# Top-2 experts: the routing weight multiplied into the gate's activation by GpSimd, all 16 down products in one PSUM bank

## What is computed

```python
def moe(x2d, W_router, gate_w, up_w, down_w):
    logits = x2d @ W_router.T
    probs = jax.nn.softmax(logits.astype(jnp.float32), -1)
    topw, sel = jax.lax.top_k(probs, TOPK)
    topw = topw.astype(x2d.dtype)
    wmat = jnp.sum(jax.nn.one_hot(sel, E, dtype=x2d.dtype) * topw[..., None], axis=1)
    g = jnp.einsum('td,efd->tef', x2d, gate_w)
    u = jnp.einsum('td,efd->tef', x2d, up_w)
    h = jax.nn.silu(g) * u
    ye = jnp.einsum('tef,edf->ted', h, down_w)
    out = jnp.einsum('ted,te->td', ye, wmat)
    return (out, logits)
```

## Time and profile before

| what | value |
|---|---|
| median of 3 runs | 1696.12 us (1695.65 to 1700.82) |
| profiled execution, its own time | 1696.32 us |
| span from first to last instruction | 1694.5 us |
| mean granted TensorE clock | 0.826 of full speed |
| TensorE matmul busy | 1251.0 us (74%) |
| VectorE busy | 1175.1 us (69%) |
| ScalarE busy | 606.9 us (36%) |
| GpSimd busy | 395.3 us (23%) |

### The profile page before, as it was taken

How to read it: one execution, slowest core, us unless ns; L and a number is a source line. 1 busy time by engine, 2 the same in 40 slices (tenths; PEclk the granted TensorE clock), 3 DMA queues, 4 the chain that set the end, 5 groups by cost and what they waited for, 6 DMA issues and landing times.

```text
span 1694.5 us, 13336 instructions
## 1 busy us (share of the span) xinstructions
PE 1251.0 (74%) x4026; PEld 619.1 (37%) x4026; DVE 1175.1 (69%) x2595; ACT 606.9 (36%) x1086; POOL 395.3 (23%) x284
## 2 busy tenths in 40 slices
PE   2222775966487675967696887878889789999897
PEld 1001332332233222343232553635547345555554
DVE  6897798878987898847547688696785752444321
ACT  1510652236322642224232331412233325764543
POOL 5232042312422142211103223030320111111211
PEclk8555886979697986969797679797787989999999
DMA  5000000000000000020001000000000010000000
GB/s 178 0 0 0 1 1 0 1 0 1 0 1 1 0 0 1 1 85 1 1 0 56 1 1 0 1 1 1 1 1 1 0 56 1 7 1 7 1 7 7
DMA packets 11271, 17.78 MB, mean 10 GB/s; under 512 B 1304, under 2 KB 7584, under 8 KB 10688
## 3 DMA queue, kind: packets, MB, share of 16 engines
q1 hardware_dynamic: 11200, 16.93, 2.9%
HBM read 15.88 MB, written 1.05 MB: 10 GB/s over the span
## 4 chain that ended last, share of the span: by engine, by line
PE 33%; DVE 14%; ACT 4%; issue 2%; POOL 1%; POOLq 0%; DVEq 0%; ACTq 0%
PE bankE L1659 7%; PE bankE L1737 4%; PE bankE L1149 4%; PE bankE L1132 3%; DVE b_yt L1454 2%; PE bankE L1151 1%; PE bankS L1701 1%; PE bankE L518 1%; PE bankS L1686 1%; ACT b_pr L1046 1%; DVE c_tw L1829 1%; PE bankE L544 1%; DVE b_xnS L1236 1%; PE bankE L1134 1%; DVE b_pT L1426 1%
## 5 line engine op out<-in xcount | busy, mean ns | idle before, releaser
L284 POOL TENSOR_TENSOR cv<-cv,hc 128x1024 f32<-128x1024 f32 x60 | 141.4, 2357 | 303.9 <-DVE hc L683 303.6
L676 DVE TENSOR_TENSOR_SCAN hs<-dA,carry,dbx 128x512 f32<-128x512 f32 x128 | 186.0, 1493 | 3.9 <-ACT dA L358 0.5
L1659 PE MATMUL bankE<-c_h,c_w 128*128 128x512 f32 x288 | 151.7, 609 | 9.5 <-DVE c_tw L1829 6.6
L1632 ACT ACTIVATE c_h<-bankE,C 128x512 f32<-128x512 f32 x144 | 98.9, 688 | 117.4 <-PE bankE L1737 117.2
L395 ACT ACTIVATE sg<-bankE,C 128x512 f32<-128x512 f32 x80 | 54.9, 687 | 172.5 <-PE bankE L518 172.5
L1829 DVE SCALAR_TENSOR_TENSOR c_tw<-bankE,C,wb_ready 128x512 f32<-128x512 f32 x32 | 24.0, 750 | 130.0 <-PE bankE L1659 130.0
L449 PE MATMUL bankS<-bc,sel 96*128 96x512 bf16 x64 | 30.5, 476 | 102.5 <-DVE hc L683 89.5
L1737 PE MATMUL bankE<-c_fH,c_w1H 128*128 128x512 f32 x144 | 100.8, 700 | 0.0
L1046 ACT ACTIVATE b_pr<-bankE,b_nm 128x160 f32<-128x160 f32 x128 | 48.4, 404 | 139.3 <-DVE b_nm L1415 139.3
L1149 PE MATMUL bankE<-b_kTt,b_qT 64*128 64x160 f32 x256 | 85.9, 424 | 9.4 <-ACT b_pr L1046 8.8
L358 ACT ACTIVATE dA<-dl,Aneg 128x512 f32<-128x512 f32 x128 | 81.1, 709 | 26.6 <-DVE hs L676 26.4
(11 more groups left out here) (478 smaller groups left out, 2829.3 us busy)
## 6 DMA issues: line engine op xcount, KB each, us to landing
c_w<-in_w SPq DMA_DIRECT2D x1, 2304.0 KB, 8.7
X<-in_x SPq DMA_DIRECT2D x4, 256.0 KB, 3.8
wg<-in_gate_T SPq DMA_DIRECT2D x1, 1024.0 KB, 7.9
wu<-in_up_T SPq DMA_DIRECT2D x1, 1024.0 KB, 10.0
f<-in_w SPq DMA_DIRECT2D x1, 1024.0 KB, 7.3
out<-X SPq DMA_DIRECT2D x4, 256.0 KB, 2.3
b_wq<-in_Wqkv SPq DMA_DIRECT2D x1, 768.0 KB, 4.9
g<-in_sw SPq DMA_DIRECT2D x2, 256.0 KB, 3.5
```

The costliest lines, as they stand in the source:

```text
L284: pool.tensor_tensor(cv[:, :, :], cv[:, :, :], hc[:, k % 2, :, :], ALU.add).then_inc(s["y_acc"], 1)
L676: V.tensor_tensor_scan(hs[:, h, :], dA[:, (HV * k + h) % DA, :], dbx[:, h, :], carry[:, k, h:h + 1], ALU.mult, ALU.add).then_inc(s["scan_d ...
L1632: act.activation(h[:, n % 3, :], E[k % 2][:, :], ACT.Gelu_apprx_tanh, bias=col("b1_3", k)).then_inc(s["c_h"], 1)
L1659: pe.matmul(E[2][:, :], w2[:, k, :], h[:, n % 3, :], start=(f == 0), stop=(f == FB3 - 1)).then_inc(s["c_down"], 1)
```

## The change

- `weigh`, `add`, the tile tw and the semaphore tw_ready are gone. GpSimd multiplies each of the 16 blocks' sg with its expert's wb in place, piece by piece, and signals sw_ready; VectorE's hh now waits for sw_ready in place of sg_ready.
- sg has three buffers in place of two. ScalarE writes wb for expert x once GpSimd has multiplied all blocks up to expert x-2.
- TensorE accumulates all 16 down products in E[2], and ScalarE copies the sum to acc in L1.
- ORDER is written anew from aA0.1 on, in all stages. The pieces are the same ones.
- Six waits and signals that ran on semaphores of their own now count on shared ones (acts_const, x2_done, b_cst, b_room), with the counts raised to match.

The order around the M blocks, old and then new (expert groups 0, 1, 2 and the tail):

```diff
@@ -93,49 +93,49 @@
...
-    aA0.1 an0.1 ao0.1 aM5.0 aN1.1 aM6.0 an1.1 aM7.0 ao1.1 aM8.0 aN2.1 aM9.0 an2.1 ao2.1 aN3.1 aA1.1 an3.1 ao3.1 aM10.0 aN4.1 aM11.0 an4.1
-    ao4.1 aM12.0 aN5.1 aM13.0 an5.1 aM14.0 ao5.1 aM15.0 aN6.1 aL1.0 an6.1 aA2.1 aL3.0 ao6.1 aL4.0 aN7.1 aL5.0 an7.1 aR2.0 ao7.1 aR5.0 aN8.1
...
-    aF3.2 aM1.1 aM2.1 aF8.2 aF4.2 aF9.2 aM3.1 aM4.1 aN0.2 aA0.2 an0.2 ao0.2 aM5.1 aN1.2 aM6.1 an1.2 aM7.1 ao1.2 aM8.1 aN2.2 aM9.1 an2.2
-    ao2.2 aM10.1 aN3.2 aM11.1 aA1.2 an3.2 ao3.2 aN4.2 an4.2 ao4.2 aM12.1 aN5.2 aM13.1 an5.2 aM14.1 ao5.2 aM15.1 aN6.2 an6.2 aL1.1 aA2.2
...
-    aF1.3 aR1.2 aF5.3 aR3.2 aF6.3 aF2.3 aF0.3 aR4.2 aF7.3 aM0.2 aF3.3 aM1.2 aM2.2 aF8.3 aF4.3 aF9.3 aM3.2 aM4.2 aN0.3 aA0.3 an0.3 ao0.3
-    aM5.2 aN1.3 an1.3 aM6.2 ao1.3 aM7.2 aN2.3 an2.3 ao2.3 aN3.3 aA1.3 an3.3 ao3.3 aM8.2 aN4.3 aM9.2 an4.3 aM10.2 ao4.3 aM11.2 aN5.3 an5.3
...
-    aU18.2 aU19.2 aB1.3 aL2.2 aL6.2 aB3.3 aB4.3 aB2.3 aL7.2 bP0.0 aR1.3 aR3.3 bP1.0 aR4.3 aM0.3 aM1.3 bP2.0 bP3.0 bP4.0 bK1.0 aM2.3 aM3.3
-    bK11.0 aM4.3 aM5.3 bK2.0 bK3.0 bK13.0 aM6.3 aM7.3 bK4.0 aM8.3 aM9.3 bK14.0 aM10.3 bK5.0 aM11.3 bK8.0 aM12.3 bK15.0 aM13.3 aM14.3 aM15.3
...
+    aA0.1 an0.1 ao0.1 aM5.0 aN1.1 aM6.0 aM7.0 an1.1 aM8.0 ao1.1 aM9.0 aN2.1 aM10.0 aM11.0 an2.1 aM12.0 ao2.1 aM13.0 aN3.1 aM14.0 aM15.0
+    aL1.0 aA1.1 an3.1 aL3.0 ao3.1 aL4.0 aN4.1 aL5.0 an4.1 aR2.0 ao4.1 aR5.0 aN5.1 aR6.0 an5.1 ao5.1 aU0.0 aN6.1 an6.1 aU1.0 aA2.1 ao6.1
...
+    aF7.2 aM0.1 aF3.2 aM1.1 aM2.1 aF8.2 aF4.2 aF9.2 aM3.1 aM4.1 aN0.2 aA0.2 an0.2 ao0.2 aM5.1 aN1.2 aM6.1 an1.2 aM7.1 ao1.2 aN2.2 an2.2
+    aM8.1 ao2.2 aN3.2 aA1.2 an3.2 ao3.2 aM9.1 aN4.2 aM10.1 an4.2 aM11.1 ao4.2 aM12.1 aN5.2 aM13.1 an5.2 aM14.1 ao5.2 aN6.2 an6.2 aM15.1
...
+    aB2.2 aF1.3 aF5.3 aF6.3 aF2.3 aF0.3 aL7.1 aF7.3 aR1.2 aF3.3 aF8.3 aR3.2 aR4.2 aF4.3 aF9.3 aM0.2 aM1.2 aN0.3 aA0.3 an0.3 ao0.3 aM2.2
+    aN1.3 aM3.2 an1.3 aM4.2 ao1.3 aM5.2 aN2.3 aM6.2 aM7.2 an2.3 aM8.2 ao2.3 aN3.3 aA1.3 an3.3 aM9.2 aM10.2 ao3.3 aN4.3 aM11.2 an4.3 aM12.2
...
+    aU16.2 aU17.2 aB1.3 aB3.3 aB4.3 aU18.2 aU19.2 aB2.3 bP0.0 aL2.2 aL6.2 bP1.0 aL7.2 bP2.0 bP3.0 bP4.0 bK1.0 aR1.3 bK11.0 aR3.3 bK2.0 aR4.3
+    bK3.0 bK13.0 aM0.3 aM1.3 aM2.3 aM3.3 aM4.3 aM5.3 aM6.3 aM7.3 aM8.3 aM9.3 aM10.3 aM11.3 aM12.3 aM13.3 bK4.0 aM14.3 aM15.3 bK14.0 aL1.3
...
```

The rest of the diff; the renamed semaphores of stages b and c are of the same kind as the ones in `scalar`:

```diff
@@ -210,10 +210,10 @@
...
     c3 = sb2("c3", [E1N, G], BF16)
-    sg = sb2("sg", [P, 2, G])
+    SG = 3
+    sg = sb2("sg", [P, SG, G])
     hh = sb2("hh", [P, 2, G])
     wb = sb2("wb", [P, 2, G])
-    tw = sb2("tw", [P, 2, G])
     acc = sb2("acc", [P, G])
@@ -284,12 +284,10 @@
...
                 power("s_var", "s_pow", powS, rsS, i, 2, 3)
-            elif p[0] == "M" and int(p[1:]) % FB0 == FB0 - 1:
-                x_ = int(p[1:]) // FB0
-                if x_ > 0:
-                    add(e, x_ - 1)
-            elif p == "L1":
-                add(e, E0N - 1)
+            elif p[0] == "M":
+                at_least(pool, s["sg_ready"], e, N_M, k + 1)
+                at_least(pool, s["wb_ready"], e, E0N, k // FB0 + 1)
+                pool.tensor_tensor(sg[:, k % SG, :], sg[:, k % SG, :], wb[:, k // FB0 % 2, :], ALU.mult).then_inc(s["sw_ready"], 1)
             elif p == "L3":
@@ -297,25 +295,16 @@
...
-        def add(e, x_):
-
-            at_least(pool, s["tw_ready"], e, E0N, x_ + 1)
-            if x_ == 1:
-                pool.tensor_tensor(acc[:, :], tw[:, 0, :], tw[:, 1, :], ALU.add).then_inc(s["acc_done"], 1)
-            elif x_ > 1:
-                at_least(pool, s["acc_done"], e, E0N - 1, x_ - 1)
-                pool.tensor_tensor(acc[:, :], acc[:, :], tw[:, x_ % 2, :], ALU.add).then_inc(s["acc_done"], 1)
-
         return piece
...
         act.wait_ge(s["ld_x"], 32)
-        act.activation(Aneg[:, :], col("A_log", 0, HV * NS), ACT.Exp).then_inc(s["act_self"], 1)
-        act.wait_ge(s["act_self"], 1)
+        act.activation(Aneg[:, :], col("A_log", 0, HV * NS), ACT.Exp).then_inc(s["acts_const"], 1)
+        act.wait_ge(s["acts_const"], 1)
         act.activation(Aneg[:, :], Aneg[:, :], ACT.Copy, scale=-1.0).then_inc(s["acts_const"], 1)
         act.activation(sb2sum[:, :], col("sb2", 0), ACT.Identity, bias=col("sb2", 1)).then_inc(s["acts_const"], 1)
-        act.wait_ge(s["acts_const"], 2)
+        act.wait_ge(s["acts_const"], 3)
         act.wait_ge(s["consts"], 4)
@@ -371,13 +360,15 @@
...
                     at_least(act, s["wbc_ready"], e, E0N, x_ + 1)
-                    if x_ >= 2:
-                        at_least(act, s["tw_ready"], e, E0N, x_ - 1)
+                    at_least(act, s["sw_ready"], e, N_M, max(0, FB0 * (x_ - 1)))
                     act.activation(wb[:, x_ % 2, :], E[3][:, :], ACT.Copy).then_inc(s["wb_ready"], 1)
                 at_least(act, s["g_ready"], e, N_M, k + 1)
-                if k >= 2:
-                    at_least(act, s["hh_ready"], e, N_M, k - 1)
-                act.activation(sg[:, k % 2, :], E[0][:, :], ACT.Silu).then_inc(s["sg_ready"], 1)
+                if k >= SG:
+                    at_least(act, s["hh_ready"], e, N_M, k - SG + 1)
+                act.activation(sg[:, k % SG, :], E[0][:, :], ACT.Silu).then_inc(s["sg_ready"], 1)
+            elif p == "L1":
+                at_least(act, s["down"], e, N_M, N_M)
+                act.activation(acc[:, :], E[2][:, :], ACT.Copy).then_inc(s["acc_done"], 1)
             elif p == "L5":
@@ -493,7 +484,7 @@
...
                 down0(e, N_M - 1)
-                at_least(pe, s["acc_done"], e, E0N - 1, E0N - 1)
+                at_least(pe, s["acc_done"], e, 1, 1)
                 at_least(pe, s["sg_ready"], e, N_M, N_M)
@@ -531,11 +522,8 @@
...
         def down0(e, b):
-            x_ = b // FB0
             at_least(pe, s["hh_ready"], e, N_M, b + 1)
-            if b % FB0 == 0 and x_ > 0:
-                at_least(pe, s["tw_ready"], e, E0N, x_)
-            mm = pe.matmul(E[2][:, :], wd[:, b, :], hh[:, b % 2, :], start=(b % FB0 == 0), stop=(b % FB0 == FB0 - 1))
+            mm = pe.matmul(E[2][:, :], wd[:, b, :], hh[:, b % 2, :], start=(b == 0), stop=(b == N_M - 1))
             mm.then_inc(s["down"], 1)
@@ -726,15 +714,11 @@
...
             elif p[0] == "M":
-                at_least(V, s["sg_ready"], e, N_M, k + 1)
+                at_least(V, s["sw_ready"], e, N_M, k + 1)
                 at_least(V, s["u_ready"], e, N_M, k + 1)
...
                     at_least(V, s["down"], e, N_M, k - 1)
-                V.tensor_tensor(hh[:, k % 2, :], sg[:, k % 2, :], EU[k % 2][:, :], ALU.mult).then_inc(s["hh_ready"], 1)
-                if k % FB0 == 0 and k > 0:
-                    weigh(e, k // FB0 - 1)
-            elif p == "L1":
-                weigh(e, E0N - 1)
+                V.tensor_tensor(hh[:, k % 2, :], sg[:, k % SG, :], EU[k % 2][:, :], ALU.mult).then_inc(s["hh_ready"], 1)
             elif p == "L3":
@@ -829,13 +813,6 @@
...
             V.tensor_tensor(w3[64:72, :], wrr[0:8, :], wtt[0:8, :], ALU.subtract).then_inc(s[ready], 1)
-
-        def weigh(e, x_):
-            at_least(V, s["down"], e, N_M, FB0 * (x_ + 1))
-            at_least(V, s["wb_ready"], e, E0N, x_ + 1)
-            if x_ >= 2:
-                at_least(V, s["acc_done"], e, E0N - 1, max(1, x_ - 2))
-            V.tensor_tensor(tw[:, x_ % 2, :], E[2][:, :], wb[:, x_ % 2, :], ALU.mult).then_inc(s["tw_ready"], 1)
```

More of the change, by code:

```diff
@@ new lines @@
+    aL3.3 bK5.0 bK8.0 aL4.3 aL5.3 bK15.0 aR2.3 bK16.0 bK7.0 bK9.0 bK6.0 aR5.3 aR6.3 aU0.3 bK10.0 aU1.3 aU2.3 aU3.3 aU4.3 bK17.0 aU5.3 aU6.3
+    aU7.3 aU8.3 aU9.3 aU10.3 aU11.3 aU12.3 aU13.3 aU14.3 bK1.1 aU15.3 bK11.1 aU16.3 bK2.1 bK3.1 bK13.1 bK4.1 aU17.3 aU18.3 aU19.3 aL2.3
+    aL6.3 bK14.1 bK5.1 aL7.3 bD0.0 bA0.0 bK8.1 bA10.0 bQ0.0 bQ1.0 bK15.1 bQ2.0 bK16.1 bQ3.0 bK7.1 bK9.1 bK6.1 bK10.1 bC0.0 bK17.1 bK1.2
+    bK11.2 bN0.0 bC1.0 bV0.0 bH0.0 bK2.2 bK3.2 bN1.0 bK13.2 bW0.0 bO0.0 bC2.0 bV1.0 bH1.0 bK4.2 bW1.0 bO1.0 bN2.0 bC3.0 bV2.0 bH2.0 bW2.0
@@ new lines @@
+    bX2.1 bX3.1 bX4.1 bX5.1 bX6.1 bX7.1 bA2.1 bK6.3 bC0.2 bK10.3 bA13.1 bN0.2 bC1.2 bV0.2 bH0.2 bK17.3 cI0.0 cQ0.0 bN1.2 bW0.2 bO0.2 bC2.2
+    bV1.2 bH1.2 bW1.2 cG0.0 bO1.2 bN2.2 bC3.2 bV2.2 bH2.2 bW2.2 cQ1.0 bN3.2 bO2.2 bA0.3 bV3.2 bH3.2 bW3.2 bA10.3 cG1.0 bO3.2 cS2.0 bQ0.3
+    bA1.2 bQ1.3 bQ2.3 bQ3.3 bA11.2 bA12.2 cH0.0 cZ0.0 cZ1.0 bA3.2 cE0.0 bX0.2 bX1.2 bX2.2 bX3.2 bX4.2 bX5.2 bX6.2 bX7.2 bA2.2 cZ2.0 cE1.0
+    bC0.3 cS3.0 cT0.0 bA13.2 ct0.0 cS4.0 bN0.3 cZ3.0 cE2.0 bC1.3 bV0.3 bH0.3 bN1.3 cE3.0 cT1.0 bW0.3 ct1.0 bO0.3 bC2.3 bV1.3 bH1.3 cT2.0
@@ new lines @@
+    bW1.3 ct2.0 bO1.3 bN2.3 bC3.3 bV2.3 bH2.3 cS5.0 cT3.0 bW2.3 bN3.3 ct3.0 bO2.3 bV3.3 bH3.3 cZ4.0 bW3.3 bO3.3 bA1.3 bA11.3 bA12.3 cY0.0
+    cy0.0 bA3.3 cW0.0 cZ5.0 cE4.0 cS6.0 bX0.3 cV0.0 cZ6.0 cT4.0 bX1.3 bX2.3 ct4.0 cZ7.0 cE5.0 bX3.3 bX4.3 cX0.0 bX5.3 bX6.3 cT5.0 bX7.3
+    cS7.0 ct5.0 bA2.3 cE6.0 cT6.0 bA13.3 cI1.0 ct6.0 cR0.0 cE7.0 cT7.0 ct7.0 cR1.0 cR2.0 cY1.0 cR3.0 cU0.0 cy1.0 cU1.0 cU2.0 cU3.0 cS8.0
+    cW1.0 cU4.0 cV1.0 cX1.0 cU5.0 cQ0.1 cU6.0 cU7.0 cU8.0 cU9.0 cU10.0 cG0.1 cU11.0 cQ1.1 cG1.1 cU12.0 cH0.1 cZ0.1 cZ1.1 cU13.0 cE0.1 cU14.0
```

(10 more changed lines are left out.)

74 lines of the change are left out of this document (28 added, 46 removed).

## The result

The changed kernel takes 1759.57 us (median of 4, 1755.48 to 1766.99) against 1695.88 us for the kernel before on the same chip: ratio 1.0378, 95% interval 1.0329 to 1.0426. The forecast was 1690 us in a range of 1673 to 1709, with 0.28 on slower.

A forecast was written before the change was run, and what follows sets the result against it. No engine is full: VectorE's queue holds M steps, the TensorE, ScalarE, VectorE loop U steps. Groups -4.6 and tail -1.7, later stages nothing, sum to -6.3 us from 1696.3: 1690 us, range 1673 to 1709.

The forecast's parts named there:

- TensorE alone hides this: Expert blocks: each hh ready about 1.35 us later, covered by TensorE's block spacing of 2.57 to 2.8 us.
- six places behind an addition: Mamba groups 1 to 3, M right behind an o: VectorE idles 3.8 us each, making a step 10.6 us.
- The gain from tw: Beside the scans: 24 of 32 removed tw at 0.60 us each free at most 14.4 us of VectorE.
- the third rival: Whole kernel: waits for sw_ready replace the 14.4 us freed and U steps keep 7.85 us; 1696 us, chance 0.15.
- The step sum: Mamba groups 1 to 3, state steps counted at estimated prices: -2, +1 and -3.6, together -4.6 us.
- Group 1's three packed steps: Mamba group 1, 11 blocks in three steps: 35.8 us against 21.9, +13.9, less 2.1 for L3.
- The giving back in steps 5 to 14: Mamba group 1, ten steps with sparse U blocks: 63.2 us against 76.9, -13.7.
- Group 2's six M steps: Mamba group 2, first six state steps: 50.5 us against 43.8, +6.7.
- Group 3's five: Mamba group 3, first five state steps: 49 us against 36.5, +12.5.
- Later stages: I count nothing, with 5 us either way: Stages after the tail: same instructions in slightly other places, counted at zero, 5 us either way.
- The first rival: M steps: GpSimd takes over as the bound; 1701 to 1713, say 1707 us, chance 0.25.
- The rule that I weighed: Beside scans: two-SBUF-input VectorE and SBUF-reading GpSimd instructions exclude each other; 36 full holds would add 46 us (1736).

The follow-up runs named there:

- the old order: The changed kernel's code with the ORDER of before in all stages, against the kernel before: 1737.76 us (1.0208 to 1.0331).
- Taking TensorE's waits away: Changed code with the ORDER of before, plus down products two blocks behind their gate and three hh buffers: 1738.79 us, against 1737.76 without these.
- the accumulation alone: Changed code with the ORDER of before, without any multiplication by the routing weight, hh waiting for silu: 1691.23 us (0.9942 to 0.9997 against the kernel before).

## Why the prediction was wrong

**"TensorE alone hides this" failed.** It was said of the 1.35 us by which each hh is later. It holds in the tail, where VectorE has little else: ten hh from 816.20 to 840.25, 2.67 us apart, each after a wait of about 2 us that costs nothing: from group 3's end to xnE it takes 109.7 us with the new code and with the old code in the same order, 2.0 more than before (forecast -1.7). Beside the scans it fails. I put the cost at six places behind an addition, 3.8 us each, 23 us in all and partly counted already; the trace has 43 waits and 92 us. TensorE's pace decides when silu is done; but what stands behind the waiting hh is VectorE's dbx and scans, on the engine that is the bound, and they pay, whatever covers the wait on TensorE: in the old order VectorE's waits at hh grew from 40 to 115 us and the time by 44. Taking TensorE's waits away gave nothing back; taking hh one place later gave 30, a short multiplication 30, both 63. The size, 6 places and 23 us, was wrong with it.

**The gain from tw was counted in full at 0.60 each.** 14.4 us were "at most"; the accumulation alone gave 2 us in time by the medians, 5 by the ratio (0.5 to 10), and 2.7 in the three groups, less than such sums vary. With tw gone, hh waits for silu and TensorE instead (63 us in that kernel, 40 before). In this the third rival, "nothing follows", was right about the code's other half.

**The step sum.** Group 1's three packed steps were priced 35.8 and took 45.8, with the old code 41.2: the step with M14, M15, L1, L3 and L4 takes 15.8 (19.4 with the old code) where I put 12.7, since L1 to L4 is a chain over four engines and not 2.1 us of VectorE work. Steps 0 and 4 I left out; they cost 2.6 and 4.6 more. The giving back in steps 5 to 14 came out near (-15.9 against -13.7), but by luck: the ten steps were priced 76.9 before and 63.2 after and took 92.0 and 76.1. Both sums left out the L and R pieces, and it is these moving out that shortened the steps; single-block U steps took 5.8 to 8.2, not 5.9. Group 2's six M steps, 50.5, took 52.0; but its other steps, priced 6 us shorter, came out 2.6 longer. Group 3's five, 49, took 54.5, against 34.6 before where I had 36.5.

**"Later stages: I count nothing, with 5 us either way" failed most plainly.** They cost 29 us in the changed kernel. I took the same instructions in slightly other places as the same work; the diff showed K pieces ahead of attention pieces and I didn't ask who stands behind them on TensorE.

**The first rival** (GpSimd as bound, 1707) named the right engine with the wrong mechanism as sized. The rule that I weighed, the Trainium skill's "SBUF — State Buffer", section "Who interferes with whom", is borne out in kind with hh later (scans of 1403 ns with the narrow multiplication, 1490 with the full one), but that is 11 us for all 64 multiplications, where I had 46 by the rule for the 36 beside scans. With hh at its place the scans take 1400 ns with the full, the narrow and no multiplication: few of them meet one, since VectorE stands while GpSimd multiplies. In the changed kernel they got shorter than before, with GpSimd's 28 additions to acc gone. The length of a link in a chain counts even where nothing collides: 30 us in the old order.

Right were: POOL's +45 us, waits of 2 to 4 us at hh (4.0 the longest), and the warning that later stages moving by more than 5 us would make it wrong altogether.
